# The source ids of the first groups as the first loads of two layers, and the third layer's clears on VectorE instead of POOL

## The reference

```python
x = _layernorm(x + _L0_gnn_ref(x, edge_index, edge_attr_3, mu, sigma, W, b))
x = _layernorm(x + _L1_gnn_ref(x, edge_weight, edge_attr_3, edge_index, w1, b1, w2, b2))
x = _layernorm(x + _L2_gnn_ref(x, edge_index, edge_attr_32, W1, b1, W2, b2))
x = _layernorm(x + _L3_gnn_ref(x, src, dst))
```

```python
# second layer (_L1_gnn_ref): a small MLP of the edge's weight makes R, one weight matrix per edge
R = relu(abs_distances[:, None] @ w1 + b1) @ w2 + b2
Y = spherical_harmonics(rel_vec)
Fj = features[src]
...  # products of R, Y and Fj make msg
out = out.at[dst].add(msg)

# third layer (_L2_gnn_ref)
e_feat = concatenate([x[src], x[dst], edge_attr], axis=-1)
h = relu(e_feat @ W1 + b1)
v = h @ W2 + b2
x_cand = segment_max(v, dst, num_segments=num_nodes)
return maximum(x_cand, x)
```

## Time and profile before

| what | value |
|---|---|
| median of 3 timed runs | 19952.7 us |
| lowest and highest | 19945.88 and 19960.17 us |
| span of the profiled execution, which is its own time | 22392.1 us |
| instructions in it | 339145 |
| busy: PE, VectorE, ACT, POOL | 64%, 51%, 14%, 53% |
| mean granted TensorE clock | 0.744 of full speed |

### The profile page before, as it was taken

One profiled execution on the slowest core, in us unless ns is written; L12 is line 12 of the kernel. 1 busy time (PEld: TensorE's weight loads), 2 busy tenths in 40 slices (PEclk: granted clock), 3 DMA queues, 4 the chain that ended last, 5 costly groups with the idle time before them and its releaser, 6 DMA issues. The chain is left out here.

```text
span 22392.1 us, 339145 instructions
## 1 busy us (share of the span) xinstructions
PE 14372.6 (64%) x117015; PEld 8020.7 (36%) x117015; DVE 11320.3 (51%) x19882; ACT 3023.5 (14%) x4899; POOL 11821.0 (53%) x10067
## 2 busy tenths in 40 slices
PE   0565555555546677676776445555555559999999
PEld 0344333333333444444444211222121224554554
DVE  2665444444436777777777622232222344555554
ACT  0222222222211111111111001111111100000000
POOL 4788888888865555555555466666666510000000
PEclk6655555555557888888888666666666679999999
DMA  7344444444442222222222133333333335555555
GB/s 260 49 38 38 38 37 39 37 36 37 38 36 46 47 50 47 48 48 47 49 49 49 24 64 70 72 70 72 70 72 72 66 95 171 196 201 197 197 199 178
DMA packets 3739984, 1818.35 MB, mean 81 GB/s; under 512 B 2905649, under 2 KB 3513466, under 8 KB 3720410
## 3 DMA queue, kind: packets, MB, share of 16 engines
q1 hardware_dynamic: 1739132, 1336.93, 21.3%
q0 software_dynamic: 669312, 166.80, 9.2%
q10 hardware_dynamic: 1330528, 300.35, 7.3%
HBM read 1474.42 MB, written 392.90 MB: 83 GB/s over the span
## 5 line engine op out<-in xcount | busy, mean ns | idle before, releaser
L1926 POOL DMA_INDIRECT xg<-d_tab,s_i x3136 | 3265.9, 1041 | 2592.0 <-POOLq L1921 1470.4
L2827 PE MATMUL pacc<-nodes,HB 128*32 128x512 fp8e4 x70560 | 3931.5, 380 | 159.5 <-PEq L2871 158.7
L2450 POOL DMA_INDIRECT xg<-d_tab,s_i x3136 | 3006.6, 959 | 1912.3 <-POOLq L2446 966.4
L2172 PE MATMUL pR<-w,H 128*128 128x384 f32 x6272 | 2692.5, 557 | 1576.7 <-PEq L2166 987.1
L1378 POOL DMA_INDIRECT d_acc<-T,ix x1568 | 2474.7, 1578 | 524.2 <-issue 442.9
L1378 POOL DMA_INDIRECT d_acc<-AG,ix x1568 | 2469.5, 1575 | 527.0 <-issue 467.2
L2827 PEld LDWEIGHTS pacc<-nodes,HB 128*32 128x32 bf16 x70560 | 1893.6, 97 | 2070.6 <-issue 174.7
L2478 DVE TENSOR_TENSOR_SCAN U<-mU,U,up 128x512 f32<-128x512 f32 x392 | 501.6, 1280 | 3375.8 <-DVEq L2477 2772.5
L2172 PEld LDWEIGHTS pR<-w,H 128*128 128x128 f32 x6272 | 1207.8, 212 | 2693.9 <-issue 2324.2
L2601 PE MATMUL hb<-U,Wbc 128*128 128x512 f32 x784 | 655.8, 932 | 2210.9 <-PEq L2595 2103.5
L1731 PE MATMUL pm<-ms,eq 128*128 128x32 f32 x6272 | 1364.5, 399 | 935.5 <-PEq L1729 930.2
(11 more groups left out here) (338 smaller groups left out, 17940.7 us busy)
## 6 DMA issues: line engine op xcount, KB each, us to landing
packed<-d_A SPq DMA_DIRECT2D x420, 1792.0 KB, 7.8
row<-d_m SPq DMA_DIRECT2D x1568, 64.0 KB
wrow<-d_w SPq DMA_DIRECT2D x196, 512.0 KB
xg<-d_tab,s_i POOLq DMA_INDIRECT x6272
d_scan<-so ACTq DMA_DIRECT2D x392, 256.0 KB
d_A<-stage ACTq DMA_DIRECT2D x97, 784.0 KB, 11.0
d_ea<-in_ea_t ACTq DMA_DIRECT2D x1, 50176.0 KB
d_exp<-T ACTq DMA_DIRECT2D x1, 50176.0 KB, 250.1
```

Source lines behind the costliest of these rows:

```text
L1926: e.indirect_dma_start(out=xg[k][:, t, :], out_offset=None, in_=d_tab, in_offset=bass.IndirectOffsetOnAxis(ap=s_i[n][:, t:t + 1], axis=0)) ...
L2172: last = e.matmul(pR[u % 2][:, j, 0:384], H[k][:, (2 * u + j) * P:(2 * u + j + 1) * P], w2[:, :], start=True, stop=True)
L2450: e.indirect_dma_start(out=xg[n][:, j * ST + c, :], out_offset=None, in_=d_tab, in_offset=bass.IndirectOffsetOnAxis(ap=s_i[d][:, col:col + ...
L2827: end = e.matmul(pacc[k][32 * g:32 * (g + 1), :], HB[i][:, b0 + bb, 32 * h:32 * (h + 1)], of, start=(begins and h == 0), stop=(ends and h ...
```

## The change

It has two parts.

In layer 2, SP loads the ids of the first three groups before it waits for `wz` and loads the weights. The first three calls of `load` then leave the ids out. Later calls are as before. Everything else in the layer is unchanged.

In layer 3, SP loads the ids of the first four groups before it waits for `zero`. `load` is split into `load_sources` (ids) and `load_rows` (masks and flags). The eleven clears go from the start of POOL's program to the start of VectorE's, which adds one to `zero`. No instruction is added or dropped.

```diff
--- before.py
+++ after.py
@@ -1867,6 +1867,14 @@
                         e.sem_inc(S(f"fl{n}"), 1)
                         e.sem_inc(S(f"fw{n}"), 1)
                         e.sem_inc(S(f"fe{n}"), 1)
+
+                    def load_sources(a_, n):
+                        e.wait_ge(S(f"fl{n}"), 1)
+                        e.sem_inc(S(f"fl{n}"), -1)
+                        load_src(e, s_i[n][:, :], a_, n).then_inc(S(f"li{n}"), 16)
+
+                    for n in range(3):
+                        load_sources(0, n)
                     e.wait_ge(S("wz"), 1)
                     e.sem_inc(S("wz"), -1)
                     for dst, name in ((w2, "w2m"), (w2x, "w2x"), (cm, "cm"), (cx, "cx")):
@@ -1874,22 +1882,21 @@
                     e.dma_start(w1c[:, :], a["w1"].rearrange("a h -> h a")).then_inc(S("lw"), 16)
                     e.dma_start(b1c[:, :], a["b1"].rearrange("(h a) -> h a", a=1)).then_inc(S("lw"), 16)
 
-                    def load(a_, n):
+                    def load(a_, n, sources=True):
                         s = a_ * 4 + n
                         e.wait_ge(S(f"fw{n}"), 1)
                         e.sem_inc(S(f"fw{n}"), -1)
                         e.dma_start(wrow[n][:, :].rearrange("h (c n) -> h c n", c=ST), bc(w_v[:, bass.ds(s * SW, SW)], 0, 64)
                                     ).then_inc(S(f"w{n}"), 16)
-                        e.wait_ge(S(f"fl{n}"), 1)
-                        e.sem_inc(S(f"fl{n}"), -1)
-                        load_src(e, s_i[n][:, :], a_, n).then_inc(S(f"li{n}"), 16)
+                        if sources:
+                            load_sources(a_, n)
                         e.wait_ge(S(f"fe{n}"), 1)
                         e.sem_inc(S(f"fe{n}"), -1)
                         e.dma_start(e9[n][:, :, :, :].rearrange("p k t i -> p (k t i)"),
                                     d_fr[bass.ds(s + 4, 1), :, :].rearrange("a p x -> (a p) x")).then_inc(S(f"le{n}"), 16)
 
                     for n in range(3):
-                        load(0, n)
+                        load(0, n, sources=False)
                     with e.Fori(0, G // 4 - 1) as it:
                         for n in range(4):
                             load(it + (n + 3) // 4, (n + 3) % 4)
@@ -2356,6 +2363,14 @@
                         e.sem_inc(S(f"fl{d}"), 1)
                     for n in range(DEEP):
                         e.sem_inc(S(f"fw{n}"), 1)
+
+                    def load_sources(a_, d):
+                        e.wait_ge(S(f"fl{d}"), 1)
+                        e.sem_inc(S(f"fl{d}"), -1)
+                        e.dma_start(s_i[d][:, :].rearrange("p (c t) -> p c t", c=ST),
+                                    src_v[bass.ds(a_, 1), :, :, :].rearrange("a p c t -> (a p) c t")).then_inc(S(f"li{d}"), 16)
+
+                    load_sources(0, 0)
                     e.wait_ge(S("zero"), 1)
                     e.sem_inc(S("zero"), -1)
                     for c in range(2):
@@ -2370,11 +2385,7 @@
                     e.dma_start(b2r[:, :], rows(a["L2b2"], P)).then_inc(S("lb"), 16)
                     load_init(e, [U[1][c // 2][F * (c % 2):F * (c % 2 + 1), SW - 1:SW] for c in range(ST)])
 
-                    def load(a_, d):
-                        e.wait_ge(S(f"fl{d}"), 1)
-                        e.sem_inc(S(f"fl{d}"), -1)
-                        e.dma_start(s_i[d][:, :].rearrange("p (c t) -> p c t", c=ST),
-                                    src_v[bass.ds(a_, 1), :, :, :].rearrange("a p c t -> (a p) c t")).then_inc(S(f"li{d}"), 16)
+                    def load_rows(a_, d):
                         for c in range(ST):
                             e.dma_start(mU[d][F * (c % 2):F * (c % 2 + 1), c // 2, :], rows(m_v[c, bass.ds(a_ * 4 * SW, 4 * SW)], F)
                                         ).then_inc(S(f"mr{d}"), 16)
@@ -2399,14 +2410,15 @@
                     e.sem_inc(S("past_" + e.engine.name), 1)
                     e.wait_ge(S("copies_ea"), 16)
                     e.sem_inc(S("past_" + e.engine.name), 1)
-                    load(0, 0)
+                    load_rows(0, 0)
                     for w in range(4):
                         load_edges(0, w)
 
                     def chunk(c, n, at):
                         for d in range(2):
                             count_load(e, A, at, n, d)
-                            load((c - MID) * 2 + 1 + d, 1 - d)
+                            load_sources((c - MID) * 2 + 1 + d, 1 - d)
+                            load_rows((c - MID) * 2 + 1 + d, 1 - d)
                             for w in range(4):
                                 load_edges((c - MID) * 2 + 1 + d, w)
 
@@ -2424,15 +2436,6 @@
 
                 @block.gpsimd
                 def _(e):
-                    clear = [Wbc[:, :], Wa[:, :], W2[:, :]]
-                    for q in range(2):
-                        clear += [mU[d][64:P, q, :] for d in range(2)]
-                        clear += [U[k][q][64:P, SW - 1:SW] for k in range(2)]
-                    for part in clear:
-                        e.memset(part, 0.0).then_inc(S("pc"), 1)
-                        e.wait_ge(S("pc"), 1)
-                        e.sem_inc(S("pc"), -1)
-                    e.sem_inc(S("zero"), 1)
                     count_start(e, A)
                     for n in range(DEEP):
                         e.sem_inc(S(f"fxg{n}"), 1)
@@ -2464,6 +2467,15 @@
 
                 @block.vector
                 def _(e):
+                    clear = [Wbc[:, :], Wa[:, :], W2[:, :]]
+                    for q in range(2):
+                        clear += [mU[d][64:P, q, :] for d in range(2)]
+                        clear += [U[k][q][64:P, SW - 1:SW] for k in range(2)]
+                    for part in clear:
+                        e.memset(part, 0.0).then_inc(S("vc"), 1)
+                        e.wait_ge(S("vc"), 1)
+                        e.sem_inc(S("vc"), -1)
+                    e.sem_inc(S("zero"), 1)
                     begin["dve"](e)
                     e.wait_ge(S("init"), 64)
                     e.sem_inc(S("init"), -64)
```

## The result

| | before | changed |
|---|---|---|
| median of 20 timed runs | 19955.06 us | 19922.1 us |
| lowest and highest | 19945.88, 19966.57 | 19909.72, 19927.24 |
| profiled span | 22392.1, and 19953.9 in a second profile | 19919.8 |

The ratio is 0.9983, with an interval of 0.9976 to 0.9989: 33 us less by the medians, 22 to 48 by the interval.

A forecast was written before the change was run, and what follows sets the result against it. Layer 2 was taken as bound by VectorE and layer 3 by POOL, each from its first group. 19952.7 - 11.2 - 20.9 = 19920.6 us, predicted as 19921, range 19897 to 19956.

The forecast's parts named there:

- The two terms: Starts of layers 2 and 3: first gathers come earlier and the time falls with them, -11.2 and -20.9 us.
- The bounds: In timed runs layer 2 goes at VectorE's pace, 21.9 us per group, layer 3 at POOL's, 20.0, from their first groups.
- The profile itself costs time: Whole kernel: the profiled span of 22392.1 us against timed 19952.7 leaves 2439 us that exist only under the profile.
- The cover in layer 2: Layer 2's start: H is finished before the first group's sixteenth gather, so the whole 11.2 us passes to VectorE.
- The price at nothing: VectorE's clears beside gathers in layers 2 and 3 cost 0; the rival, clears stop gathers, +10.5 us, 19931, chance 0.07.
- The crawl: Rival, layer 3's start: SP's loads beside gathers take 3.3 us each, second ids come late, 20008 us; chance 0.07.
- the missing 2352 us: Layers 2 and 3: 1372 + 980 us saved at both layers' least paces, taken as nearly all the profile's extra time.
- More than the sum: Rival, layer 3's start: the earlier start absorbs POOL's 17.38 us stall, 19903, with a second such stall 19886; chance 0.14.

The follow-up runs named there:

- the halves: Each layer's part of the change alone, other layer as before: layer 2's part 19937.89 us (0.9995 of before), layer 3's part 19925.75 us (0.9989).
- the list three times: Changed kernel with VectorE's eleven clears in layer 3 done three times: 22358.6 us (1.0 of before), run again 22388.74 us (0.9985).
- the clears of H eight times: Changed kernel with the two clears of H in layer 2 done eight times: 22336.28 us (0.9988 of before), run again 22401.85 us (0.9985).

## Why the prediction was right

**The two terms.** "First gather 6771.7, 11.2 us earlier" and "first gather 20.9 us earlier": by rows of the same kind of execution, 11.3 and 20.8. By time, 11.0 and 23.1 for the halves, 33.0 together against 32.1. That the time came within 1 us is in part luck: the interval alone is 26 us wide, and the median of before that the sum starts from moved by 2.4 us with more runs. The shifts of the gathers are what was right. Taking layer 3's 2.76 us from issue to gather for layer 2 as well was right: SP issues 0.51 us behind the clear, and the gather is there 2.89 us later.

**The bounds.** "In a timed run layer 2 goes at VectorE's pace and layer 3 at POOL's, each counted from its first group": 21.9 and 20.0 us were worked out, 22.1 and 20.15 measured, and the lengths of both did not change with the start. In layer 3 the gathers moved 20.8 us and `xp` 6.9, and the time followed the gathers. For layer 2 VectorE's 0.98 speaks, but POOL is as near: 3346.1 busy and 883.1 of `issue` are 4229 of 4333 us, 21.6 per group. The 20.0 that I gave POOL there missed that its gathers stretch beside VectorE (below). Which of the two carries layer 2's shift is not shown.

**The step that failed, without harm,** is "The profile itself costs time". The second profile of before has a span of 19953.9, and all runs of two sets took 22.4 ms, those of the kernel before among them. The missing 2439 us belong to a kind of execution, in which both engines wait, and not to the profiling. Of them 1470.4 - 228.8 us are POOL's waits at `L1921` and 966.4 - 65.7 at `L2446`, by the lines' views in the two profiles of before. (Each of these two lines stands behind two waits in the kernel, for the ids and for a free `xg`, so the name alone doesn't tell which one it was.) The arithmetic that used them (busy share times pace, and the issue rate) held since it rests on what the engines have to do, which is nearly the same in both: VectorE has 21.9 us of work per group of layer 2 in the one and 0.98 x 22.1 = 21.6 in the other. What puts an execution into one kind or the other no run shows. But for the one of 21.42 ms, each of the three sets was of one kind, and each was taken on another chip, so the chip is one candidate; it was not tested.

**The cover in layer 2** did not hold whole. "the whole 11.2 us passes to VectorE": `hp` moved 9.75. It used to start 2.6 us behind the sixteenth gather and now starts 4.1 behind it. The loads next to it are a reason that fits the rows. These are the DMA engines' busy tenths, in 40 slices, from 6755 to 6790 us of the profile after and from 6751 to 6791 of the second profile of before:

```profile
DMA  0005300166316999999999999999310110118960
...
DMA  0000000640399999999999997011000110001110
```

After, they are full from 6766 to 6779.5 us, with four `wrow` of 512 KB, and the sixteenth gather starts at 6778.2, while they are. Before, they were full to about 6775, and the sixteenth gather started at 6785.4. The gathers' packets go through the same engines (in the window after, SP's queue took 51.7% of the 16 engines' time and the gathers' 7.5%). That the late data comes from this is not shown: loading the second to fourth `wrow` after the first group's gathers was not tried.

**The price at nothing.** Clears beside gathers: 0, as taken; the list took 11.2 us for my 12.1. The Trainium skill ("SBUF — State Buffer", Who interferes with whom) says so for a VectorE instruction with at most one SBUF input outside the two-port modes, and the rows agree with it: 0.94 to 0.97 us per gather. What its box on the "DVE blocks DMA" trap describes did not happen beside these clears.

**The crawl,** given 0.07, is not in the executions of 19.9 ms: after the change SP issues its first 12 weight DMAs in 6.2 us beside gathers, and the second ids go out at 48.8 us, in time for 83. That the slow issues had to do with the missing 2352 us was right; they come with that kind of execution, and there the second ids came late, as told above. The 3.3 us per DMA that I took was too much even there, and part of such spacing is in the record and not in the issue (last section).

**More than the sum** needed a stall like the 17.38 us of the earlier trace rows in the timed runs. In the second profile of before and in the one after, POOL stands nowhere for more than 0.31 us between two gathers in the first 450 us of layer 3, so there was none to absorb.

## What to carry to other kernels

Where a stage is bound by one engine at a constant rate from its first to its last item, as layer 3 is by POOL at 19.9 ms, anything that lets that engine's first item start earlier is worth its full length once. A later start of all others should then be free until a buffer or an input of the bound engine runs out: count that point (here the 65th gather, 80 us), and leave room, since with the list three times the input came 27 us later than counted. Before a difference between a profile and the timed runs is put down to the profiling, take a second profile. Put the loads that the bound engine waits for first, but see also what large loads beside them do to the data that it fetches.

## What the runs showed of the hardware

Gathers stretch beside a VectorE instruction with two inputs in SBUF (`Q`, `e`) and not beside one with one of its two in PSUM (`pR`). In the profile after, VectorE and POOL in layer 2:

```profile
8008.98 0.67 DVE L2001 TENSOR_TENSOR AG<-pR,FG 128x512 f32<-128x512 f32 x1
8009.20 0.95 POOL L1933 DMA_INDIRECT xg<-d_tab,s_i  x1 [0.31 <-issue]
...
8015.08 1.34 DVE L2025 TENSOR_TENSOR tv<-Q,e 128x1152 f32<-128x1152 f32 x1
8015.44 1.80 POOL L1933 DMA_INDIRECT xg<-d_tab,s_i  x1 [0.30 <-POOLq L1932]
```

From the stretched gather to the start of the next are 2.10 us, otherwise 1.25. The mean gather of layer 2 takes 1067 ns and that of layer 3 955, with the same median of 944; the difference is 3136 x 0.112 = 351 us of POOL's time in layer 2. It costs only as far as POOL bounds that layer. The same section of the Trainium skill says that a VectorE instruction with two SBUF inputs contends with a GpSimd one that reads SBUF; the 1.80 us agree.

In executions of 22.4 ms SP's rows stand 1.05 to 3.3 us apart per DMA beside gathers, mostly from 22 us behind the first gather on, and 0.4 to 0.6 where POOL stands still; at 19.9 ms they stand 0.4 to 0.6 apart in either case, but for the loads of `ef`. Not all of that spacing is issue time, for the rows themselves come late. In the second profile of the clears of H eight times, POOL's 65th gather of layer 3, the first that needs the second ids, and SP's row of the load of these ids:

```profile
13045.53 0.95 POOL L2453 DMA_INDIRECT xg<-d_tab,s_i  x1 [0.30 <-issue]
13046.06 0.70 SPq L2370 DMA_DIRECT2D s_i<-d_src  x1
```

The gather starts 0.53 us ahead of the row of the load that it waits for, where the first gathers of layer 3 start 2.76 to 2.89 us behind the row of their ids; so this row is some 3.3 us late or more. Where POOL stands until the ids land, as in 51.72 and 19.15 us above, the row is in its place, and the stall itself shows that the load was late. The granted clock of PE in layer 2 was 0.87 at 22.4 ms and 1.00 at 19.9 ms.
